# A graph network's last edge stage: 144 edge columns made by TensorE in place of 112

## The reference

```
W   = einsum('rb,bio->rio', comp, basis)        # 64 relations, each 64 x 64
msg = node_feats[src] * norm                    # norm: one weight per edge
s   = segment_sum(msg, etype * N + dst)         # per relation and node
h   = relu(einsum('rni,rio->no', s, W) + bias)  # = sum over edges of norm * (x[src] @ W[etype])
y   = h + relu(node_feats @ res_w.T + res_b)
out = (y - mean) * rsqrt(var + eps) * gamma + beta
```

## Time and profile before

| | us |
|---|---|
| median of 3 runs | 5953.28 (5952.83 to 5963.26) |
| span of the profiled execution, first to last instruction | 5023.8 |
| whole time of the profiled execution | not on the page |
| runs' median less that span | 929.5 |
| last edge stage, within the span | 4096 to 4950 |

### The profile page before, as it was taken

How to read it: one execution, slowest core, us unless ns; L and a number is a source line. 1 busy time by engine, 2 the same in 40 slices (tenths; PEclk the granted TensorE clock), 3 DMA queues, 4 the chain that set the end, 5 groups by cost and what they waited for, 6 DMA issues and landing times. The chain is left out here.

```text
span 5023.8 us, 55747 instructions
## 1 busy us (share of the span) xinstructions
PE 3828.8 (76%) x16477; PEld 2687.1 (53%) x16477; DVE 4001.3 (80%) x5661; ACT 2076.3 (41%) x3728; POOL 3704.0 (74%) x3415
## 2 busy tenths in 40 slices
PE   1677777762999999999999947888883666677651
PEld 1344444432888888888888843333331443333321
DVE  3788888874899999999999856899996657677763
ACT  0577777751344444444444423444443322222221
POOL 6777777764788888888888637777776567777774
PEclk6899999985999999999999957899996778888875
DMA  8777887764788888888888643444443662222221
GB/s 304 261 274 277 283 282 281 281 213 141 281 326 316 320 322 317 325 314 328 316 320 323 250 93 111 131 131 131 132 129 99 240 248 66 72 68 72 66 62 44
DMA packets 359919, 1074.05 MB, mean 214 GB/s; under 512 B 101414, under 2 KB 124642, under 8 KB 315300
## 3 DMA queue, kind: packets, MB, share of 16 engines
q1 hardware_dynamic: 240788, 850.33, 44.9%
q0 software_dynamic: 103232, 158.19, 12.5%
q10 hardware_dynamic: 15696, 63.31, 3.1%
HBM read 677.98 MB, written 392.57 MB: 213 GB/s over the span
## 5 line engine op out<-in xcount | busy, mean ns | idle before, releaser
L1859 PE MATMUL COLS<-CF,XF 128*128 128x256 f32 x6272 | 1485.6, 380 | 6.2 <-DVE XF L1967 6.2
L1859 PEld LDWEIGHTS COLS<-CF,XF 128*128 128x128 f32 x6272 | 1135.0, 190 | 130.4 <-DVE XF L1967 6.6
L1135 ACT ACTIVATE OUT<-SC 128x576 f32<-128x576 f32 (+3 forms) x392 | 576.9, 1472 | 1082.2 <-DVE SC L1070 722.1
L1826 POOL DMA_INDIRECT G<-x_tab,SRC x784 | 835.7, 1066 | 229.1 <-issue 216.4
L1018 POOL DMA_INDIRECT G<-xl_tab,SRC x752 | 728.3, 969 | 229.2 <-issue 223.4
L1018 POOL DMA_INDIRECT G<-rel_tab,REL x672 | 641.5, 955 | 205.0 <-issue 205.0
L1018 POOL DMA_INDIRECT G<-kv_tab,SRC x640 | 628.6, 982 | 195.0 <-issue 193.5
L1444 PE MATMUL PICK<-HOT,KV 125*128 125x512 bf16 x2700 | 629.2, 397 | 132.4 <-ACT TURNED L1476 117.8
L1608 PE MATMUL MADE<-XM,W 128*128 128x512 f32 x896 | 484.6, 699 | 163.7 <-DVE XM L1696 163.6
L1444 PEld LDWEIGHTS PICK<-HOT,KV 125*128 125x128 bf16 x2700 | 272.2, 101 | 482.6 <-issue 179.6
L1262 PE MATMUL WK<-W,HT 128*128 128x256 f32 x1568 | 443.8, 409 | 0.0
(11 more groups left out here) (307 smaller groups left out, 6763.3 us busy)
## 6 DMA issues: line engine op xcount, KB each, us to landing
SHB<-ea9t SPq DMA_DIRECT2D x196, 1024.0 KB, 9.6
wkv_tab<-WKV SPq DMA_DIRECT2D x98, 1024.0 KB, 6.1
WKV<-wkv_tab SPq DMA_DIRECT2D x98, 1024.0 KB, 5.9
scan<-OUT SPq DMA_DIRECT2D x196, 288.0 KB
scan<-OUT ACTq DMA_DIRECT2D x98, 576.0 KB
rel_tab<-YS SPq DMA_DIRECT2D x50, 1024.0 KB, 12.6
RAW<-spread SPq DMA_DIRECT2D x196, 256.0 KB, 2.8
spread_q<-ZQ SPq DMA_DIRECT2D x98, 512.0 KB
```

Source lines behind the costliest of these rows:

```text
L1135: nc.scalar.activation(self.OUT[d][:, :, 0:WD], SC[b][:, 0:WD, 1:1 + C].rearrange("p r j -> p j r"), ACT.Copy).then_inc(self.copied_out, 1)
L1826: pool.indirect_dma_start(out=e.G[0][b][:, col, :], out_offset=None, in_=x1_tab, in_offset=bass.IndirectOffsetOnAxis(ap=SRC[:, at:at + 1], ...
L1859: nc.tensor.matmul(acc, XF[b][:, k, edges_], CF[:, k, :], start=(k == 0), stop=False)
```

## The change

The last edge stage makes 18 batches of eight columns, 144 in place of 112, and gathers 640 columns of `rel_tab` in place of 672. The masks are spread over the same 88 chunks, so a batch spans five chunks, one of them (batch 9) four. The node rows of 14 batches still come from the 112 gathers into `XG`. Those of the batches 5, 9, 13 and 17 (`PICKED3`) are picked in the stage itself: the node table is split into bf16 pieces (`X3`: high, middle, low, and a blank fourth, 25 blocks of nodes by two products), VectorE compares the 25 blocks of node numbers with 512 sources in five groups of five (`compare`), TensorE multiplies (`pick`, ten products a group), ScalarE copies the half batch out (`take_half`), and the batch's `turn` is two products with `FOLD`, which adds up the pieces. A group's compare stands ahead of the mask, and its pick behind the multiply, that `PICK_BEFORE` names.

To make room, the edge weights move into the PSUM tensor of the messages (448 columns behind the 576), and the types, their upper halves and codes have one buffer instead of two, so `take` of a batch is followed by `read_types` of the next batch, not the one after it.

```diff
-BATCHES3 = 14
+BATCHES3 = 18
+PICKED3 = [5, 9, 13, 17]
...
+GATHERED3 = [i for i in range(BATCHES3) if i not in PICKED3]
+GATHERED_COLS = [MADE_COLS[8 * i + q] for i in GATHERED3 for q in range(8)]
+HALVES3 = [(i, h) for i in PICKED3 for h in range(2)]
+PICK_BEFORE = {16 * (i - 5) + 14 + 5 * g + 4 * (g >= 5): 10 * n + g for n, i in enumerate(PICKED3) for g in range(10)}
+CHUNK_OF = {g: max(t for t in range(NCH) if MASKS_AT[t] <= j) for j, g in PICK_BEFORE.items()}
...
-                        for j, (t, c) in enumerate(MADE_COLS):
+                        for j, (t, c) in enumerate(GATHERED_COLS):
...
+                if layer == 3:
+                    sums_and_weights = ctx.enter_context(nc.psum_tensor(unique("MSG"), [P, 1024], F32))
+                    self.MSG = sums_and_weights[:, 0:R * (1 + C)].rearrange("p (r j) -> p r j", j=1 + C)
+                    self.EW = sums_and_weights[:, R * (1 + C):R * (1 + C) + 56 * C]
...
-                TYPE8 = e.pair("TYPE8", [P, 8 * P], I32)
-                UPPER, CODE = e.pair("UPPER", [P, 8 * P]), e.pair("CODE", [P, 8 * P])
+                TYPE8 = sb("TYPE8", [P, 8 * P], I32, ctx)
+                UPPER, CODE = sb("UPPER", [P, 8 * P], F32, ctx), sb("CODE", [P, 8 * P], F32, ctx)
...
+                        def load_half(h):
+                            wait(sp, narrowed, h)
+                            sp.dma_start(SRC_HALF[:, :], src_half[h:h + 1, :].to_broadcast([P, 512]))\
+                              .then_inc(src_half_in, 16)
...
+                        nc.gpsimd.iota(NODE[:, :], [[1, K]], base=0, channel_multiplier=K).then_inc(blank, 1)
+                        nc.gpsimd.memset(X3[:, :, 1, 64:128], 0.0).then_inc(blank, 1)
...
                         def turn(i):
-                            wait(pe, doubled, i + 1)
                             wait(pe, masked, MASKS * i)
+                            if i in PICKED3:
+                                wait(pe, half_taken, 2 * PICKED3.index(i) + 2)
+                                for h in range(2):
+                                    ins = nc.tensor.matmul(XT8[:, 512 * h:512 * h + 512],
+                                                           FOLD[:, :, :].rearrange("p a f -> p (a f)"),
+                                                           PICKED[:, 512 * h:512 * h + 512], start=True, stop=True)
+                                ins.then_inc(x_turned, 1)
+                                return
+                            wait(pe, doubled, GATHERED3.index(i) + 1)
...
+                        def pick(g):
+                            h, part = divmod(g, 5)
+                            wait(pe, compared, g + 1)
+                            if part == 0:
+                                wait(pe, half_taken, h)
+                            for k in range(5 * part, 5 * part + 5):
+                                for piece in range(2):
+                                    ins = nc.tensor.matmul(PICK[:, :], X3[N, k, piece, :], HOT[g % 2][N, k % 5, :],
+                                                           start=(k == 0 and piece == 0),
+                                                           stop=(k == K - 1 and piece == 1))
+                            ins.then_inc(picked, 1)
...
                                 multiply(i, c)
+                                if MASKS * i + c in PICK_BEFORE:
...
+                                    pick(PICK_BEFORE[MASKS * i + c])
...
+                        def narrow(h):
+                            wait(act, src_half_in, (h + 1) * 16)
+                            wait(act, compared, 5 * h)
+                            nc.scalar.activation(ID16[:, :], SRC_HALF[:, :], ACT.Copy).then_inc(narrowed, 1)
+
+                        def take_half(h):
+                            i, half = HALVES3[h]
+                            wait(act, picked, 5 * h + 5)
...
+                            nc.scalar.activation(PICKED[:, 512 * half:512 * half + 512], PICK[:, :], ACT.Copy)\
+                              .then_inc(half_taken, 1)
...
+                        def compare(g):
+                            h, part = divmod(g, 5)
...
+                            wait(v, narrowed, h + 1)
+                            wait(v, picked, g - 1)
+                            for k in range(5 * part, 5 * part + 5):
+                                ins = nc.vector.tensor_scalar(HOT[g % 2][N, k % 5, :], ID16[N, :], NODE_F[N, k:k + 1],
+                                                              None, ALU.is_equal)
+                            ins.then_inc(compared, 1)
...
                                     take(i)
-                                    if i + 2 < BATCHES3:
-                                        read_types(i + 2)
+                                    if i + 1 < BATCHES3:
+                                        read_types(i + 1)
                             for j in range(MASKS_AT[t], MASKS_AT[t + 1]):
+                                if j in PICK_BEFORE:
+                                    compare(PICK_BEFORE[j])
                                 mask(j)
```

More of the change, by code:

```diff
@@ L872, in __init__ @@
                 self.BR = sb("BR", [P, H, 1 + C], F32, ctx)
-                if layer != 1:
+                if layer in (0, 2):
                     self.T1 = sb("T1", [P, C, self.FE], F32, ctx)
@@ L1561, in edges_3 @@
                 XT8, MADE = (ctx.enter_context(nc.psum_tensor(unique(name), [P, 1024], F32)) for name in ("XT8", "MADE"))
-                BACK = e.bank("BACK")
-                type8_in = [e.sem(f"type8_in{b}") for b in range(2)]
+                BACK, PICK = e.bank("BACK"), e.bank("PICK")
+                X3 = sb("X3", [P, K, 2, 128], BF16, ctx)
+                FOLD, NODE, NODE_F = sb("FOLD", [P, 2, 64], F32, ctx), sb("NODE", [P, K], I32, ctx), sb("NODE_F", [P, K], F32, ctx)
+                SHARED = sb("SHARED", [P, 3584], F32, ctx)
+                HOT = [SHARED[:, 1280 * b:1280 * b + 1280].bitcast(BF16).rearrange("p (k n) -> p k n", k=5) for b in range(2)]
+                REST = SHARED[:, 0:K * 64].rearrange("p (k f) -> p k f", k=K)
+                PICKED = SHARED[:, 2560:3584]
+                SRC_HALF, ID16 = sb("SRC_HALF", [P, 512], I32, ctx), sb("ID16", [P, 512], U16, ctx)
+                src_half_in = e.sem("src_half_in")
+                narrowed, compared, picked, half_taken = (e.sem("narrowed"), e.sem("compared"), e.sem("picked"),
+                                                          e.sem("half_taken"))
+                x_high, x_rest, x_middle, x_low, blank, folds = (e.sem("x_high"), e.sem("x_rest"), e.sem("x_middle"),
+                                                                 e.sem("x_low"), e.sem("blank"), e.sem("folds"))
+                type8_in = e.sem("type8_in")
                 numbered, weights_made, halved, coded = (e.sem("numbered"), e.sem("weights_made"), e.sem("halved"),
@@ L1623, in _ @@
                         wait(pe, weights_made, 4)
+                        wait(pe, folds, 2)
                         for i in range(BATCHES3):
@@ L1646, in place @@
                                   .then_inc(placed, 1)
[L1648 removed]
+                        def narrow(h):
[5 more added lines that the diff above has]
+                            wait(act, picked, 5 * h + 5)
+                            if h == 0:
+                                wait(act, x_low, 1)
+                            if h >= 2 and half == 0:
+                                wait(act, x_turned, PICKED3[h // 2 - 1] + 1)
+                            nc.scalar.activation(PICKED[:, 512 * half:512 * half + 512], PICK[:, :], ACT.Copy)\
+                              .then_inc(half_taken, 1)
+                        wait(act, xg_in, 16 * 8 * len(GATHERED3))
                         double(0)
                         double(1)
+                        nc.scalar.activation(X3[:, :, 0, 0:64], X[:, :, :], ACT.Copy).then_inc(x_high, 1)
                         wait(act, e.ready, e.N_READY)
@@ L1655, in step @@
                             for i in range(2, BATCHES3):
-                                if t == LAST_MASK[i - 2] + 2:
+                                if t == LAST_MASK[i - 2] + 2 and i in GATHERED3:
                                     double(i)
+                            if t == 1:
+                                wait(act, x_rest, 1)
+                                nc.scalar.activation(X3[:, :, 0, 64:128], REST, ACT.Copy).then_inc(x_middle, 1)
+                            for h in range(len(HALVES3)):
+                                if t == (CHUNK_OF[5 * h - 1] + 1 if h else 1):
+                                    narrow(h)
+                                if t == CHUNK_OF[5 * h + 4] + 1:
+                                    take_half(h)
                             if t + 1 < NCH:
@@ L1702, in take @@
                             wait(v, turned_back, i)
-                            nc.vector.scalar_tensor_tensor(out=TURNED[:, :], in0=UPPER[i % 2][:, :],
```

(9 more changed lines are left out.)

61 lines of the change are left out of this document (37 added, 24 removed).

## The result

The changed kernel takes 6065.84 us (median of 4 runs, 6060.67 to 6066.74) where the kernel of before took 5954.41 beside it. The ratio is 1.0178, with a 95% interval of 1.0164 to 1.0193: slower by 1.8%, some 106 us (the two medians themselves are 111 apart). The prediction was 6028 us, range 5970 to 6095.

What follows compares the result with a forecast made beforehand. Gathers bound the kernel before; after, VectorE with TensorE would. First `TURNED` 4165.5 + 737 - 7 + 53 + 21 = 4969.5, last sums at 5013.5, 69 us later; scaled to 75, this gave 6028 us, range 5970 to 6095.

Steps and rivals of the forecast that it cites:

- The gathers set the pace: Last edge stage before the change: GpSimd's 672 gathers never wait for another engine, 1.26 us each, 8.57 us a chunk.
- Up to the first `TURNED`: Start of the last edge stage: first `TURNED` at 4165.5 us, before at 4178.42, as the first batch ends with chunk 3.
- From the first to the last: Steps between batches: 737 us, 7 less for the last hand-over, plus 53 of compares and 21 of picks.
- The end: Last gathers run at 1.26 us: last sums start about 44 us behind the last `TURNED`, before 75.
- the sign of 43.5 us: What a profile after would show: `TURNED` to `TURNED` 43.5 us in the last, unpicked batches, 46 to 50 in picked ones.
- Hand-over: At a batch's end, from the start of `XT` to `TURNED`: mean 10.45 us, on the chain of VectorE with TensorE.
- Compares and picks: Compares on VectorE between masks, 1.35 us a group, 53 us; picks on TensorE in seven hand-overs, 3 us each, 21 us.
- Layout, single buffers, ScalarE, SyncE: Weights beside messages, single type buffers, narrowing, extra loads: nothing; 40 us if VectorE waited at each group without store cover.
- my two readings: The 929 us over the span: around the program, 69 us slower; timed runs slower throughout, ratio 1.185, 82; middle 75.
- A: Rival: gathers stay the bound, with hand-over under 7 us and compare group under 0.7; 5908 to 5915 us; chance 0.10.
- B: Rival: no change to be told, within 0.2%, as more work could hold TensorE's clock at 2.4 GHz; chance 0.06.
- C: Rival: TensorE becomes the bound with picks at the low clock, 53 us a batch; 6107 to 6135 us; chance 0.09.

Runs made afterwards that it cites:

- e0: The kernel of before, unchanged, profiled again: span 5963.9 us, time 5965.72 us, last edge stage 1057.1 us.
- e8: The changed kernel with four gathers a chunk from chunk 4 on instead of six or seven: 5852.58 us, ratio to before 0.9774.
- e1: The changed kernel with the next batch's turn behind a batch's last multiply, not ahead of multiply 12: 5984.91 us, ratio to before 1.0048.
- e3: The changed kernel with one one-hot compare in each group instead of five: 6046.15 us, ratio to before 1.0154.
- e4: The changed kernel's layout with 14 batches, all of gathered node rows, no picks or compares: ratio to before 1.0007.
- e6: The changed kernel with the second half of a mask's columns multiplied for a batch's first mask only: ratio to before 1.0045.
- e11: The kernel of before with 2 batches instead of 14 and the turning back ahead of multiply 1: 5885.60 us, ratio to before 0.9791.
- e9: e1 plus GpSimd waiting, before chunk t's gathers, until masks of all chunks before t - 1 are multiplied: 6056.85 us, ratio to before 1.0121.
- e10: The kernel of before with the turn behind the last multiply and gathers in step with the multiplies: 5967.95 us, ratio to before 0.9970.

## Why the prediction was right, and where it was wrong

The mechanism it named holds: VectorE with TensorE is the chain, the gathers wait for it, compares and picks stand on it, and the layout costs nothing. The size came out 106 where I had 75, and part of the agreement is luck, since the base from which I counted was not that of the timed runs, and a wait of 217 us, that of the masks, stands in no term.

- **The bound of before.** "The gathers set the pace" is true of the first profile and wrong for the timed runs: there they wait 224 us (e0). This is the step that failed. The 40 us of removed gathers were credited as a shorter end (75 to 44 us, -31); in the runs it went from 51.4 to 45.8, -6 (last `TURNED` to last gather).
- **The terms, against e0.** Up to the first `TURNED`: -13 predicted, 118.8 to 96.2 = -23 measured. From the first to the last: +113 predicted, 886.9 to 1016.5 = +130 measured. The end: -31 and -6. Sum +69 and +101.
- **The batch.** I had (737 - 7 + 53 + 21) / 17 = 47.3 us. The kernel has 59.8, but 47.9 in e8: the chain is sized right, and 12 us of held signals stand on top. So the sign of 43.5 us in the last, unpicked batches fails (60.9 us to the last but one `TURNED`; 44.9 in e8). Before has 68.2 in place of 53.2, 15 more. As 17 x 12 and 13 x 15 are nearly equal (204 and 195), these fell out of the difference. That is the luck.
- **Hand-over.** From `XT` to `TURNED` it is 10.26 us on average in e8 (I had 10.45) and 12.0 in the changed kernel, where held signals are in it; the two rows below are a short case, 9.75. Moving the turn is worth 4.8 us a batch, not the 7 that I expected of it (e1).

```profile
5324.00 1.27 PE L1642 MATMUL XT<-IDENT,X 128*128 128x128 f32 x8 [2.21 <-DVE XM L1795]
...
5333.75 1.28 DVE L1802 SCALAR_TENSOR_TENSOR TURNED<-UPPER,CODE_OF_F,MADE 128x1024 f32<-128x1024 f32 x1 [7.29 <-PE MADE L1661]
```

- **Compares and picks.** Five compares take 1.50 us on average (60.0 us for 40 groups; the row above is a short one of 1.42), where I had 1.35. On the chain I had 53 us; by e3 it is 37 or less. Picks are then 70.5 - 37 = 34 or more where I had 21. Only their sum is well shown: 70.5, and 74 predicted.
- **Layout, single buffers, ScalarE, SyncE.** Zero, and zero by e4. `MSG` takes 1.030 us beside the weights, 1.029 before.
- **From the span to the time.** Neither of my two readings was right. The 929 us lay within the span, and not evenly: the first, third and last edge stages grew by 200 to 280 us each and the stage ahead of the last by 122 (235 to 357), the second edge stage, from first to last gather, from 1622 to 1656. The rule of the Trainium skill, Advanced Engine Details and Errata, "Clock Domains", that I quoted, would have made GpSimd's own times longer; a gather of `rel_tab` has 0.948 us in e0 and 0.955 there, so the traces do not agree with it as the cause.
- **Rivals.** A and B are out. What A feared of the compares is small: a gather that overlaps one takes 0.97 us on average (58 of them), one that overlaps no VectorE instruction 0.94, under 2 us in all. C (TensorE the bound, +154) has the right engine and the wrong reason: TensorE idles while its signals are held, and half of its products gone gave 3.9 us a batch (e6).

Open: why the signals are held, and why not in the first profile of before, whose gathers ran as densely. e8 and the stage ahead in e11 show that the waits go where the gathers thin out; e9 and e10 agree, but won nothing. No run shows which part of the chip does it, nor whether it is the gathers' issue or the data that they move. The unchanged first and third edge stages, 260 and 280 us longer than in that profile, were not tried.

## What to carry to other kernels

Before counting from a profile, compare its execution's span with the timed runs: if they differ by more than the program can have outside its span, find which gaps differ, or the bound read from it may not be theirs. A wait whose named releaser is long done is to be looked up among the semaphore events, and beside what the other engines do when it ends. Columns made by TensorE to spare gathers paid nothing here: with 2 batches in place of 14 the program is 2.1% faster (1.7 to 2.5).

## What the runs showed that I had not expected

- In every profile but the first one of before, TensorE's semaphore signals come up to 23 us late beside back-to-back gathers (in e0 a multiply that ended at 5448.3 by its rows let its mask go at 5471.3), one by one while the gathers run on, and in bunches 0.06 us apart when they stop. In the last edge stage a gather of `rel_tab` (0.955 and 0.948 us) and a `MSG` (1.029 and 1.028) take as long in both kinds of execution.
- Two profiles of one kernel: 5023.8 and 5963.9 us, with VectorE busy 4001 and 3994 us.
- Ten picks of 512 bf16 columns take 2.32 to 3.27 us in the changed kernel (2.32 in most groups), five compares of 512 columns 1.40 to 1.63 us.
